# Attention and feed-forward block on one core: a new order for the drain, a third step of fp32 products, and the last normalisation cut in two

## The reference

```
n = layernorm(x)
q, k, v = split(n @ w_qkv)          # outer column bands in fp16, middle in fp32
s = softmax(q k^T / sqrt(256))
x = x + layernorm(s v @ out_w^T + out_b)
n = layernorm(x)
xr, xk = mix of n with n shifted by one row, weights mu_r, mu_k
k = relu(xk @ W_k)^2
x = x + layernorm(sigmoid(xr @ W_r) * (k @ W_v))
```

## Time and profile before

| | us |
|---|---|
| median of 3 runs | 801.1 (798.98 to 801.8) |
| the profiled execution | 799.6 |
| its span, first to last instruction | 797.8 |
| TensorE busy in the span | 784.1 (98%) |
| VectorE / ScalarE / GpSimd busy | 647.8 / 573.5 / 529.3 |

### The profile page before, as it was taken

The page is one execution under the profiler, slowest core; times in us unless marked ns, Lnnn a source line. Parts: engine busy times, 40 slices in busy tenths (PEclk is TensorE's granted clock), DMA queues, the critical chain, the costliest instruction groups (busy, mean ns, idle before and its releaser), DMA issues.

```text
span 797.8 us, 16563 instructions
## 1 busy us (share of the span) xinstructions
PE 784.1 (98%) x5823; PEld 576.6 (72%) x5823; DVE 647.8 (81%) x1677; ACT 573.5 (72%) x791; POOL 529.3 (66%) x768
## 2 busy tenths in 40 slices
PE   8999999999999999999999999999999999999996
PEld 6556777777777777777777777777777777777884
DVE  6788888877797879888878879987778787788787
ACT  4677768777677778777668787887767676775663
POOL 3370356666767768866756776966675985677776
PEclk9999999999999999999999999999999999999999
DMA  6798789477866769867657986957876554777701
GB/s 186 158 186 125 138 159 177 87 143 147 172 119 141 148 126 189 146 126 139 94 141 157 183 156 130 138 110 145 145 140 123 108 108 106 147 146 143 149 29 40
DMA packets 348260, 108.70 MB, mean 136 GB/s; under 512 B 321937, under 2 KB 347921, under 8 KB 348177
## 3 DMA queue, kind: packets, MB, share of 16 engines
q1 hardware_dynamic: 348176, 107.64, 70.0%
HBM read 18.75 MB, written 8.39 MB: 34 GB/s over the span
## 4 chain that ended last, share of the span: by engine, by line
PE 94%; DVE 2%; DMA 0%; issue 0%; POOL 0%; POOLq 0%; ACT 0%; DVEq 0%
PE Y L1725 7%; PE Y L1729 7%; PE Y L1727 7%; PE Y L1726 7%; PE Y L1728 7%; PE S L1704 7%; PE S L1708 7%; PE S L1705 7%; PE S L1707 7%; PE S L1706 7%; PE M L1669 6%; PE M L1670 6%; PE M L1671 6%; PE M L1687 1%; PE M L1688 1%; PE M L1685 1%
## 5 line engine op out<-in xcount | busy, mean ns | idle before, releaser
L1285 DVE TENSOR_SCALAR_CACHE_REDUCE probs<-S 128x512 f32<-128x512 f32 x256 | 173.2, 677 | 65.0 <-PE S L1708 64.8
L933 ACT ACTIVATE probs<-probs,exp_bias,kappa 128x2048 f32<-128x2048 f32 x64 | 133.9, 2092 | 60.1 <-DVE exp_bias L1298 60.1
L1303 DVE TENSOR_TENSOR p_lo<-probs,p_hi 128x2048 f16<-128x2048 f32 x61 | 166.7, 2732 | 5.7 <-ACT p_hi L862 5.7
L1727 PE MATMUL Y<-pt_hi,planes 128*128 128x256 f16 x496 | 135.2, 273 | 0.0
L1725 PE MATMUL Y<-pt_hi,planes 128*128 128x256 f16 x496 | 135.2, 273 | 0.0
L1726 PE MATMUL Y<-pt_lo,planes 128*128 128x256 f16 x496 | 135.2, 273 | 0.0
L1728 PE MATMUL Y<-pt_lo,planes 128*128 128x256 f16 x496 | 135.2, 273 | 0.0
L1729 PE MATMUL Y<-pt_hi,planes 128*128 128x256 f16 x496 | 135.2, 273 | 0.0
L862 ACT ACTIVATE p_hi<-probs 128x2048 f16<-128x2048 f32 x64 | 121.4, 1897 | 8.8 <-DMA pt_hi<-p_hi 4.8
L1704 PE MATMUL S<-turned,q_hi 128*128 128x512 f16 x256 | 97.0, 379 | 1.6 <-DMA turned<-planes 1.6
L1708 PE MATMUL S<-turned,q_lo 128*128 128x512 f16 x256 | 97.0, 379 | 0.0
(11 more groups left out here) (289 smaller groups left out, 2039.9 us busy)
## 6 DMA issues: line engine op xcount, KB each, us to landing
x_res<-in_L_attn_x SPq DMA_DIRECT2D x32, 256.0 KB, 3.6
out_x<-gate SPq DMA_DIRECT2D x31, 256.0 KB, 3.2
xs<-in_L_attn_x SPq DMA_DIRECT2D x13, 512.0 KB, 4.9
pt_hi<-p_hi SPq DMA_TRANSPOSE x62, 5.0
pt_lo<-p_lo SPq DMA_TRANSPOSE x62, 4.8
xs<-in_L_attn_x SPq DMA_DIRECT2D x2, 256.0 KB, 3.8
gate<-in_L_attn_x SPq DMA_DIRECT2D x1, 512.0 KB, 6.5
att<-in_L_attn_x SPq DMA_DIRECT2D x1, 512.0 KB, 4.3
```

Source lines behind the costliest of these rows:

```text
L1285: dve.tensor_scalar(probs[:, h % 2, t, c * BLK:(c + 1) * BLK], S[k % RING][:, :], 1.0, None, ALU.mult, ALU.max, accum_out=chunk_max[:, t, ...
L1303: dve.tensor_tensor(p_lo[:, t, :], probs[:, h % 2, t, :], p_hi[:, t, :], ALU.subtract).then_inc(p_lo_made, 1)
L1727: pe.matmul(to[:, 1, :], high, p_h, start=False, stop=False, skip_group_check=True)
```

## The change

Nothing changes in the main loop. In the drain:

- FULL goes from H - 2 to H - 3, so step 29 takes fp32 products beside 30 and 31. Its split_high, split_low, sq_hi and squares_low go.
- In the last step VectorE subtracts the means alone (`attention_centre_tile`, `gate_centre_tile`), which needs no power, and one scalar_tensor_tensor then multiplies by the power and adds the residual. Before, a tensor_scalar did both steps of the norm behind the power, and a tensor_tensor the sum; for attention tile 0 the norm stood on ScalarE, and both sums stood on GpSimd.
- The lists of the drain are written in a new order on all five engines, and some calls move. From GpSimd to VectorE: squares_low of 25 and 26, split_low(26, 0) and (28, 1), add_attention of 28, differences of 28 and of the last tile, finish of 26. From VectorE to GpSimd: squares_low of 27 and 28, split_low(27, 0) and (28, 0), add_attention of 29, finish of 25. From VectorE to ScalarE: the norm of the mix of 27 and of the last tile, attention_norm of 28 and 29, gate_norm of 28; gate_norm of 26 goes the other way.

```
-    FULL = H - 2
+    FULL = H - 3
 ...
-            def attention_norm_tile(t):
-                dve.wait_ge(a_rstd_made, H + t)
+            def attention_centre_tile(t):
+                dve.wait_ge(a_moments, LAST * RT + t + 1)
                 dve.wait_ge(att_normed, LAST * RT + t)
                 o = att[:, LAST % 2, t, :]
-                dve.tensor_scalar(o, o, amv[:, t, 0:1], arstd[:, t:t + 1], ALU.subtract, ALU.mult).then_inc(att_normed, 1)
+                dve.tensor_scalar(o, o, amv[:, t, 0:1], None, ALU.subtract).then_inc(att_normed, 1)
 ...
                 dve.wait_ge(att_normed, LAST * RT + t + 1)
-                dve.tensor_tensor(res[:, LAST % 4, t, :], x_res[:, LAST % 2, t, :], att[:, LAST % 2, t, :],
-                                  ALU.add).then_inc(res_made, 1)
+                dve.wait_ge(a_rstd_made, H + t)
+                dve.scalar_tensor_tensor(out=res[:, LAST % 4, t, :], in0=att[:, LAST % 2, t, :], scalar=arstd[:, t:t + 1],
+                                         in1=x_res[:, LAST % 2, t, :], op0=ALU.mult, op1=ALU.add).then_inc(res_made, 1)
 ...
-            def gate_norm_tile(t):
-                dve.wait_ge(g_rstd_made, H + t)
+            def gate_centre_tile(t):
+                dve.wait_ge(g_moments, LAST * RT + t + 1)
                 dve.wait_ge(g_normed, LAST * RT + t)
                 o = gate[:, LAST % 2, t, :]
-                dve.tensor_scalar(o, o, gmv[:, t, 0:1], grstd[:, t:t + 1], ALU.subtract, ALU.mult).then_inc(g_normed, 1)
+                dve.tensor_scalar(o, o, gmv[:, t, 0:1], None, ALU.subtract).then_inc(g_normed, 1)
 
             def finish_tile(t):
                 dve.wait_ge(out_made, LAST * RT + t)
                 dve.wait_ge(g_normed, LAST * RT + t + 1)
-                dve.tensor_tensor(gate[:, LAST % 2, t, :], gate[:, LAST % 2, t, :], res[:, LAST % 4, t, :],
-                                  ALU.add).then_inc(out_made, 1)
+                dve.wait_ge(g_rstd_made, H + t)
+                o = gate[:, LAST % 2, t, :]
+                dve.scalar_tensor_tensor(out=o, in0=o, scalar=grstd[:, t:t + 1], in1=res[:, LAST % 4, t, :],
+                                         op0=ALU.mult, op1=ALU.add).then_inc(out_made, 1)
 ...
             turn_low(H - 2, 1)
+            store(H - 8)
+            turn_high(H - 2, 1)
+            turn_high(H - 1, 0)
             load_residual(H - 3)
-            turn_high(H - 2, 1)
-            store(H - 8)
-            turn_high(H - 1, 0)
             turn_low(H - 1, 0)
+            turn_high(H - 1, 1)
             load_residual(H - 2)
-            turn_high(H - 1, 1)
             turn_low(H - 1, 1)
 ...
             project_out(H - 4, KEYS_LEFT)
-            values(H - 3, 1, 4)
+            values(H - 3, 1, 2)
+            feed(H - 7)
+            turn_mix_in(H - 5)
+            values(H - 3, 2, 6)
             mix_keys(H - 6, 0)
+            values(H - 3, 6, 7)
             receptance(H - 6)
-            values(H - 3, 4, 5)
-            turn_mix_in(H - 5)
-            values(H - 3, 5, 8)
-            feed(H - 7)
+            values(H - 3, 7, 8)
+            feed(H - 6)
             values(H - 2, 0, 2)
```

More of the change, by code:

```diff
@@ L816, in _ @@
                         full_weight(w)
-            squares_low(H - 7)
-            res_rsqrt(H - 5, 0)
+            res_rsqrt(H - 5, H - 4)
+            att_rsqrt(H - 4, H - 3)
             split_low(H - 6, 1)
-            split_low(H - 6, 0)
-            att_rsqrt(H - 4, 0)
-            add_attention(H - 4)
             differences(H - 5)
-            res_rsqrt(H - 4, H - 4)
-            squares_low(H - 6)
+            res_rsqrt(H - 4, H - 3)
+            split_low(H - 5, 0)
             split_low(H - 5, 1)
             gate_rsqrt(H - 7, H - 6)
[L829 to L836, removed]
+            att_rsqrt(H - 3, H - 2)
+            finish(H - 7)
+            gate_rsqrt(H - 6, 0)
+            add_attention(H - 3)
+            squares_low(H - 5)
+            res_rsqrt(H - 3, H - 2)
+            split_low(H - 4, 0)
+            att_rsqrt(H - 2, H - 1)
+            gate_rsqrt(H - 5, H - 5)
             differences(H - 3)
+            res_rsqrt(H - 2, H - 1)
             finish(H - 5)
[L839 to L842, removed]
+            att_rsqrt_tile(0, 0)
+            squares_low(H - 4)
+            att_rsqrt_tile(1, 0)
+            res_rsqrt_tile(0, H - 0)
             differences(H - 2)
+            gate_rsqrt(H - 4, H - 4)
+            res_rsqrt_tile(1, H - -1)
             finish(H - 4)
[L845 to L850, removed]
             gate_rsqrt(H - 3, H - 3)
-            differences_tile(1)
             finish(H - 3)
@@ L1592, in _ @@
                         weight_low(2 * i + 1)
-            mix(H - 6, 1)
-            inverse_sums(H - 2)
             mix(H - 6, 0)
-            inverse_sums(H - 1)
+            squares_low(H - 7)
             attention(H - 4)
             attention_stats(H - 4)
-            mix_in(H - 5)
+            inverse_sums(H - 2)
+            inverse_sums(H - 1)
+            mix(H - 6, 1)
+            split_low(H - 6, 0)
             probs_low(H - 1, 0)
-            attention_norm(H - 4)
+            gated(H - 7)
@@ L1603, in _ @@
+            add_attention(H - 4)
             residual_stats(H - 4)
+            mix(H - 5, 0)
+            squares_low(H - 6)
             probs_low(H - 1, 1)
             attended_low(H - 3)
+            gated(H - 6)
             mix(H - 5, 1)
-            gated(H - 7)
             gated_stats(H - 7)
+            differences(H - 4)
             attention(H - 3)
             attention_stats(H - 3)
-            gated(H - 6)
-            mix(H - 5, 0)
-            attention_norm(H - 3)
+            mix(H - 4, 1)
@@ L1614, in _ @@
+            mix(H - 4, 0)
             gated_stats(H - 6)
-            finish(H - 7)
-            squares_low(H - 5)
-            add_attention(H - 3)
+            attended_low(H - 2)
+            gate_norm(H - 6)
             residual_stats(H - 3)
-            attended_low(H - 2)
-            mix(H - 4, 1)
-            split_low(H - 5, 0)
-            mix(H - 4, 0)
+            split_low(H - 4, 1)
             attention(H - 2)
             attention_stats(H - 2)
-            split_low(H - 4, 0)
@@ L1626, in _ @@
             gated(H - 5)
+            finish(H - 6)
             gated_stats(H - 5)
-            squares_low(H - 4)
             add_attention(H - 2)
             residual_stats(H - 2)
+            mix(H - 3, 1)
             mix(H - 3, 0)
-            mix(H - 3, 1)
+            attended_low_tile(0)
+            attended_low_tile(1)
+            attention_tile(0)
+            attention_centre_tile(0)
+            attention_tile(1)
+            add_attention_tile(0)
+            residual_stats_tile(0)
@@ L1660, in _ @@
             gated_stats_tile(1)
[L1661 removed]
+            gate_centre_tile(0)
             finish_tile(0)
[L1663 removed]
+            gate_centre_tile(1)
             finish_tile(1)
```

134 lines of the change are left out of this document (51 added, 83 removed).

## The result

| | before | after |
|---|---|---|
| median of 5 runs, us | 801.1 (798.98 to 802.63) | 796.67 (796.5 to 796.92) |
| the profiled execution / its span | 799.6 / 797.8 | 796.67 / 794.9 |
| first product of the drain to the start of the last feed | 63.36 | 61.43 |
| start of the last feed to the end of VectorE's last instruction | 4.66 | 4.18 |

The ratio is 0.9947, 95% interval 0.9935 to 0.9959: faster by 4.2 us (4.4 between the medians). The forecast was 799.7, and its range ended at 798.0. Two things are to be explained: the profiled executions differ by only 2.9 us, and the runs of before scatter over 3.65 us where those of after lie within 0.4.

The account below looks back on a forecast made before the run. TensorE, busy 98% of the span, was taken as the bound. The terms -3.5 (waits) + 1.4 (fp32) + 0.8 (feed 26) + 0.3 (late waits) - 0.4 (end) gave -1.4: 799.7 us against the median, range 798.0 to 802.6.

Parts of the forecast that it names:

- The profiled execution against the median: Whole run: the profiled execution lies 1.5 us under the median, so the forecast is 801.1 - 1.4 = 799.7.
- the floor, as TensorE's work can't shrink: Drain: with no new waits the gain is 2.6 us, 798.5, and cannot be larger; that rival's chance 0.20.
- The late waits: TensorE's end: waits before keys 30 and the keys of tiles 0 and 1 are covered by moved work, -3.5 us.
- The fp32 products: Step 29 on TensorE: fp32 keys, receptance and feed instead of split fp16 add 1.4 us.
- within the waits above: Step 29's splits that go: not on bounding engines; inputs may be late by less, counted within the 3.5 us of waits.
- The early wait: Before feed 26: TensorE waits for its late input, 0.6 to 1.0 us, taken as 0.8.
- the rival that I gave 0.19: split_low(26, 1) on GpSimd locked beside VectorE's p_lo, delaying a TensorE input by 1.47 us: 801.2; chance 0.19.
- short GpSimd work is little hit: Argument against the VectorE-GpSimd lock in the drain: short GpSimd instructions suffer little from it; no size given.
- New late waits: Last step, feed 28 and keys 30: under 0.5 us to spare, so 0.3 us of new waiting.
- The end: VectorE's last instructions: one merged instruction behind the power instead of two; gain 0.2 to 0.5 us, taken as 0.4.
- late transposes: Transpose of (30, 1) waits for store(24) to land, 3.2 us, delaying feed 26: +1.8, 802.9; chance 0.13.

Follow-up runs that it names:

- e5: Kernel before with small unread fp16 products (6, 13, 2) filling TensorE's three late waits; median 799.69 us, ratio 0.9987 to before.
- e11: e5 with 12 more small unread products ahead of the first scores; median 799.71 us, ratio 0.9993 to before.
- e4: Changed kernel with step 29 back in split fp16, the first ScalarE copy ahead of attended_high(31); median 801.44 us, ratio 1.0009 to before.
- e8: e4 with both fp16 copies placed later on ScalarE; median 799.47 us, ratio 0.9989 to before.
- e7: Changed kernel with keys 26 and receptance 26 one eighth of step 29's values later, feed 26 also later; median 796.45 us, ratio 0.9945 to before.
- e2: Kernel before with only the gate's norm and sum merged in the last step, old order kept; median 799.88 us, ratio 0.9986 to before.
- e9: Changed kernel, unchanged, profiled and timed again; median 797.34 us, ratio 0.9955 to before.
- e12: Changed kernel with 12 more small unread products ahead of the first scores; median 797.12 us, ratio 0.9963 to before.
- e1: Kernel before, unchanged, profiled and timed again; median 801.97 us, ratio 1.0007 to before.
- e6: Changed kernel with the keys of tile 0 also waiting for VectorE's gate multiplication of step 30; median 799.53 us, ratio 0.9982 to before.
- e10: e7 with 12 more small unread products ahead of the first scores; median 796.21 us, ratio 0.9946 to before.

## Why the prediction was wrong

**The profiled execution against the median.** This is the step that failed. The prediction said that the execution "is 1.5 under the median of the runs, so against the median it is 801.1 - 1.4", and so carried the 1.5 over as a constant. It was no constant: for the most part it comes from falls of the clock, which some executions have and some not, and one of the two kinds hangs on the late waits that the change removes. e5 prices that at 1.0 us (ratio 0.9987, 0.3 to 1.8 by its interval), e11, with the same filling, at 0.6 (ratio 0.9993, 0 to 1.3). For the same reason "the floor, as TensorE's work can't shrink" was none: in part of the executions the same work at half the clock took 1.5 us more. The runs of before, 798.98 to 801.8, showed the scatter, and no step asked for its cause. The sizes in the sum were off by 1.0 besides, as the terms below say; that alone would have given 798.7, inside the range.

**The late waits.** Right in place, all three gone. Of size 4.0, not 3.5: the 3.0 that the trace names, 0.65 of tails around them, and a looser row of products beside them. In before these took 1.00, 0.94 and 0.97 us from start to start, where those of after take 0.86 to 0.89:

```profile
788.14 1.03 PE L1811 MATMUL S<-turned,square 128*128 128x256 f32 x4
789.08 1.13 PE L1788 MATMUL M<-planes,mixed 128*128 128x256 f32 x4
790.05 1.03 PE L1788 MATMUL Y<-planes,mixed 128*128 128x256 f32 x4
```

**The fp32 products.** 1.23, not 1.4; right in the sum. Missed was what e4 and e8 show: with split fp16 products in the new order the old late waits go too, but new ones of 3.0 us come in their place, 2.8 of them for the low parts of step 29. The prediction put the worth of the splits that go "within the waits above".

**The early wait.** The size was right, 0.86 for 0.8, the place wrong. The landing of the transpose was not later but as early as before: p_hi started at 736.56, not 737.13, with the transpose issued behind the store at 730.63 instead of 731.12, and 0.5 of that is the earlier start of the whole drain. The store's issue took 0.69 and not the 1.15 that the prediction read. From the start of p_hi to the end of sq_hi it took 3.76, as priced. So sq_lo 26 ended at 741.14 instead of 742, and TensorE came to feed 26 at 741.25, just behind it. The wait is before keys 26, and by the mechanism of the rival that I gave 0.19: GpSimd held by VectorE. It was priced at 1.47 and is 0.86 in place of, not on top of, the other: without it TensorE would have been at feed 26 at 740.39 and, by the same rows, would have waited 0.75 there (an estimate). The forecast wait was hidden behind an unforeseen one. e7 removes both, as it moves feed 26 as well. That "short GpSimd work is little hit" was wrong: the instruction held was one of the shortest. The Trainium skill, SBUF — State Buffer, "Who interferes with whom", lets size play no part in who blocks, and the 3.24 us agree.

What counts is what stands in GpSimd's list between the held instruction and the one that TensorE needs. p_lo ended at 734.29, and split_low(26, 1) takes 1.16. Started at once it would have ended at about 735.45, in time for TensorE at 735.58 (an estimate from these rows). But a power and a shift stood ahead of it, so that it ran from 735.22 to 736.38. e4's GpSimd rows show the same from another side. There the negation got in where xm_lo ended and p_lo began, and the power behind it was held instead, 2.75 where it takes 0.69 in after:

```profile
731.21 1.04 POOL L599 TENSOR_TENSOR aminus<-zeros,amv 128x2 f32<-128x2 f32 x1
732.21 2.75 POOL L601 TENSOR_TENSOR arstd<-avar,minus_half 128x2 f32<-128x2 f32 x1
```

**New late waits.** Forecast 0.3, measured none. The mix of keys 30 ends at 778.54 and the keys start at 778.60; squares_low 28 ends 0.5 before feed 28 starts.

**The end.** Forecast 0.4, measured 0.48 in after and 0.54 in e2, with no stretching of the power: 0.56.

Together the trace gives -2.4 for a forecast of -1.4. The fall that no longer comes gives 0.6 to 1.0 more, which makes a gain of 3.0 to 3.4, beside the 3.6 of e9 and the 3.0 of e12 (ratio 0.9963). The first comparison's 4.2 to 4.4 had luck on both sides in it: the median of before was 801.1 where 92 executions give 800.6, and none of the five executions of after had a mean clock under 0.999, with a median of 796.67 where e9 has 797.34 and e12 797.12. The split into the fall and the rest is only as sharp as these intervals.

The rival "late transposes" was wrong from its first step, since the landing did not get later. Two numbers of the prediction don't come out of its own working: the bounds of the terms add up to about 799.0 to 801.3, not 798.9 to 800.7, and the late transposes lie at 802.9, above the 802.6 to which the range is said to reach them. Neither bound would have taken in the measured 796.67.

## What to carry to other kernels

When a kernel's own runs scatter by more than those of its neighbours, look for an event that comes in some executions only, and ask whether the change removes its cause; don't carry the distance from profile to median over. TensorE's wait of 1.78 us cost 1.48 more in the profile where the clock fell behind it, so its removal, or small products put into it, was worth more than the profile of an undisturbed execution says. And a product that needs no low part is to be priced by its own time and by the wait for the low part that it spares.

## What the runs showed of the hardware

- A TensorE wait of 1.78 us was followed by a fall of the clock to 0.50, for some 3.4 us in all, in e1's profile and not in the first profile of the same kernel, with the waits equal within a hundredth.
- Small products whose result nobody reads, 13 in that wait and 8 in the two beside it, lowered the median by 1.0 us in e5 and 0.6 in e11 at no cost in the drain (63.36 in all). Executions with a mean clock of 0.997 or less went from 63 of 92 to 4 of 24.
- A GpSimd instruction of 128x2 elements, 0.20 us at the median, took 3.24 in after, e6, e7, e9, e10 and e12, while VectorE ran mixes, xm_lo and p_lo, all with two SBUF inputs, one behind the other; it ended only with p_lo. In e4 and e8 it got in at one of the seams, and the power behind it was held until p_lo's end (2.75).
- An fp32 product of step 29 takes 1.73 us from start to start (eight matmul records), against 1.32 for its twelve matmuls in split fp16.
